# A test-time-training layer beside a mixture-of-experts gate on one core: expert slots spread over the scan, the first half's output norm moved into it, the ending's evacuations split

## What is computed

```
xn = layernorm(x)                                   # x: 4 x 256 tokens x 256 channels
XQ, XK, XV = xn @ q_w.T, xn @ k_w.T, xn @ v_w.T     # 32 heads of 8, minibatches of 16 tokens
# scan over 16 minibatches, carrying W1 (8x8) and b1 per batch and head
Z1 = xk @ W1 + b1
grad = ln_fused_l2_bwd(Z1, xv - xk, ln_w, ln_b)
Z1_bar = xq @ W1 - eta * tril(xq @ xk.T) @ grad + b1 - tril(eta) @ grad
W1, b1 = W1 - (last_eta * xk).T @ grad, b1 - sum(last_eta * grad)
out = xq + ln(Z1_bar)                               # per head
s = layernorm(out) * post_w + post_b, then @ o_w.T
g = silu(top-2 of 8 experts: down(up * silu(gate)))
x + s * g
```

## Time and profile before

| | us |
|---|---|
| runs, median of 3 | 278.29 (276.3 to 278.8) |
| the profiled execution, its own time | 279.46 |
| its span in the trace | 277.6 |
| VectorE busy | 211.3 (76%) |
| TensorE busy | 209.6 (75%), mean granted clock 0.865 |
| ScalarE, GpSimd busy | 138.2 (50%), 127.8 (46%) |

### The profile page before, as it was taken

One profiled execution on the slowest core, in us unless ns is written; L12 is line 12 of the kernel. 1 busy time (PEld: TensorE's weight loads), 2 busy tenths in 40 slices (PEclk: granted clock), 3 DMA queues, 4 the chain that ended last, 5 costly groups with the idle time before them and its releaser, 6 DMA issues.

```text
span 277.6 us, 5087 instructions
## 1 busy us (share of the span) xinstructions
PE 209.6 (75%) x1754; PEld 155.4 (56%) x1754; DVE 211.3 (76%) x546; ACT 138.2 (50%) x296; POOL 127.8 (46%) x173
## 2 busy tenths in 40 slices
PE   8318991069977995899299955995999799939663
PEld 6205561043656773778167643684777577828452
DVE  2999999996029499969948994959499998895312
ACT  2411663052492575187146707570567586873840
POOL 2356298066663294266226611663284373151034
PEclk9856998556999799799959997599699999986899
DMA  6992000300000300020030002000300160000011
GB/s 187 406 322 76 3 0 0 81 0 1 2 2 6 77 2 0 9 75 2 0 81 2 0 7 77 0 2 5 79 1 2 18 201 19 1 0 0 4 76 77
DMA packets 21706, 13.22 MB, mean 48 GB/s; under 512 B 10417, under 2 KB 20017, under 8 KB 21169
## 3 DMA queue, kind: packets, MB, share of 16 engines
q1 hardware_dynamic: 21168, 12.03, 14.3%
q10 hardware_dynamic: 512, 0.87, 1.0%
HBM read 11.02 MB, written 1.84 MB: 46 GB/s over the span
## 4 chain that ended last, share of the span: by engine, by line
DVE 39%; PE 34%; ACT 14%; issue 7%; POOL 2%; DMA 2%; DVEq 0%; POOLq 0%; SPq 0%; ACTq 0%
PE bank L1055 10%; DVE dW L815 5%; DVE pr L810 5%; PE bank L976 5%; PE bank L1023 4%; DVE pr L749 4%; DVE bank L760 3%; ACT L504 3%; PE bank L1129 3%; PE bank L1075 3%; ACT upw L491 2%; DVE mif L714 2%; DMA small<-in_small 2%; ACT xqm L535 2%; PE bank L1103 2%
## 5 line engine op out<-in xcount | busy, mean ns | idle before, releaser
L1023 PE MATMUL bank<-xqm,xkT 32*32 32x128 f32 x512 | 22.8, 298 | 35.5 <-ACT A L474 20.0
L320 POOL TENSOR_TENSOR hh<-gate,upw 128x256 f32<-128x256 f32 x32 | 24.2, 759 | 49.4 <-ACT upw L491 49.3
L265 POOL TENSOR_TENSOR A<-A,mask 128x256 f32<-128x256 f32 x32 | 23.4, 734 | 47.7 <-ACT A L474 47.5
L1023 PEld LDWEIGHTS bank<-xqm,xkT 32*32 32x32 f32 x512 | 13.1, 113 | 45.2 <-ACT A L474 21.6
L474 ACT ACTIVATE A<-bank,one 128x256 f32<-128x256 f32 x32 | 15.1, 473 | 46.1 <-PE bank L1023 46.0
L1075 PE MATMUL bank<-down,hT 128*128 128x256 f32 x128 | 36.6, 414 | 0.0
L784 DVE RECIPROCAL bank<-sv 128x32 f32<-128x32 f32 x16 | 5.7, 358 | 35.6 <-ACT sv L480 35.2
L1055 PE MATMUL bank<-gup_hi,xn_hi 128*128 128x512 f32 x64 | 32.5, 508 | 0.0
L1055 PE MATMUL bank<-gup_hi,xn_lo 128*128 128x512 f32 x64 | 28.1, 438 | 0.0
L1055 PE MATMUL bank<-gup_lo,xn_hi 128*128 128x512 f32 x64 | 27.9, 437 | 0.0
L1075 PEld LDWEIGHTS bank<-down,hT 128*128 128x128 f32 x128 | 24.6, 214 | 2.3
(11 more groups left out here) (149 smaller groups left out, 485.4 us busy)
## 6 DMA issues: line engine op xcount, KB each, us to landing
wblk<-w_blocks SPq DMA_DIRECT2D x8, 512.0 KB, 4.0
sgpad<-in_gup SPq DMA_DIRECT2D x1, 1024.0 KB, 9.7
G<-in_gup SPq DMA_DIRECT2D x1, 1024.0 KB, 11.7
down<-in_down SPq DMA_DIRECT2D x1, 1024.0 KB, 14.3
xkT<-in_x_bt SPq DMA_DIRECT2D x1, 1024.0 KB, 4.7
out<-G SPq DMA_DIRECT2D x4, 256.0 KB, 2.5
wkv<-in_wkv ACTq DMA_DIRECT2D x1, 512.0 KB, 4.1
x_bt<-in_x_bt SPq DMA_DIRECT2D x1, 512.0 KB, 7.6
```

Source lines behind the costliest of these rows:

```text
L320: pool.tensor_tensor(hh[:, i % 2, :, :], gate[:, i % 2, :, :], upw[:, i % 2, :, :], ALU.mult).then_inc(S_["h"], 1)
L1023: ins = pe.matmul(bk[32 * b:32 * b + 32, P * hf:P * hf + P], xkT[32 * q:32 * q + 32, hf, j, GT * b:GT * b + GT], xqm[32 * q:32 * q + 32, j ...
```

## The change

SLOTS becomes 3 slots in group 1, 5 in groups 2 to 6, 4 in group 7: all 32 stand in the scan. Every group j now begins with a slot; group_end(j-1) follows tile 1, and group_start(j) stands behind tile 4 of its own group instead of in the next. ScalarE loads the Sqrt table ahead of scores 1 and takes the first root right behind them. On GpSimd pad_grads(j-1) comes first. In the start, xn_hi is cast and the second half's queries are evacuated before any score of group 0; lower_half is one instruction of 2,048 columns instead of four of 512; mif lies in PSUM. The first half's output norm is done in fills of groups 6 and 7 on VectorE, with its row scaling on GpSimd (first_half_rows) and its roots inside ScalarE's groups 6 and 7. In the ending VectorE evacuates the first half's channels and tiles 6 and 7, ScalarE tiles 4 and 5; f_bank names banks 2, 6, 4, 5. The semaphore yT is split in yTa (ScalarE) and yTv (VectorE).

```diff
 NE, NI = 8, 128
 NF = 2 * B
 NS = NF * NE // 2
-FIRST_HALF = [0, 2, 2, 3, 3, 3, 3, 3]
...
-        mif = sb("mif", [P, NF, 2])
+        mif = bank[3][:, 488:488 + 2 * NF].rearrange("p (f k) -> p f k", k=2)
...
-            return 2 + f % 4
+            return (2, 6, 4, 5)[f % 4]
...
                 pool.wait_ge(S_["hi"], n + 1)
-                for c in range(0, 2048, 512):
-                    pool.tensor_tensor(lo[:, c:c + 512].bitcast(F32R), full[:, c:c + 512], hi[:, c:c + 512],
-                                       ALU.subtract).then_inc(S_["split"], 1)
...
             lower_half(1)
-            pool.wait_ge(S_["mask"], 1)
-            mask_scores(0, 1)
             lower_half(2)
             masked_queries(1)
-            for i in range(2, 5):
+            pool.wait_ge(S_["mask"], 1)
+            for i in range(1, 5):
                 mask_scores(0, i)
...
+            def first_half_rows():
+
+                for k in range(2):
+                    pool.wait_ge(S_["zr"], k + 1)
+                    pool.wait_ge(S_["zg"], k + 1)
+                    rows = o[:, k, :].rearrange("p (a d) -> p a d", d=HD)
+                    link(pool.tensor_tensor(rows, rows, zr[:, k, :].unsqueeze(2).broadcast_to([P, 64, HD]), ALU.mult))
+                    pool.wait_ge(S_["xqb"], 2 * B)
+                    pool.tensor_tensor(o[:, k, :], o[:, k, :],
+                                       xqb[:, 0, 2 * k:2 * k + 2, :].rearrange("p b c -> p (b c)"), ALU.add).then_inc(S_["orow"], 1)
+
...
-                    half_scale(0)
+                slots = list(range(slot, slot + SLOTS[j]))
+                slot += SLOTS[j]
+                if j == 1:
+                    hidden_product(slots.pop(0))
+                    pad_grads(0)
+                else:
+                    pad_grads(j - 1)
+                    hidden_product(slots.pop(0))
+                mask_scores(j, 1)
...
-                    mask_scores(j, 1)
-                    hidden_product(slot)
                     mask_scores(j, 2)
-                    pad_grads(j - 1)
-                    mask_scores(j, 3)
-                    hidden_product(slot + 1)
+                    hidden_product(slots.pop(0))
                 else:
...
+                    hidden_product(slots.pop(0))
+                    mask_scores(j, 2)
+                mask_scores(j, 3)
+                hidden_product(slots.pop(0))
                 mask_scores(j, 4)
...
+                if 1 < j < 6:
+                    query_bias(2 * (j - 2))
+                if j == 5:
+                    half_scale(0)
+                for i in slots:
                     hidden_product(i)
-                if j < 5:
-                    query_bias(2 * (j - 1))
-                slot += SLOTS[j]
+                if j == 6:
+                    first_half_rows()
             pad_grads(NG - 1)
-            for i in range(slot, NS):
-                hidden_product(i)
-                if i == slot:
-                    half_scale(1)
+            half_scale(1)
...
+            high_half(2)
+            queries_out(1)
+            step_std(2)
+            query_rows(0)
+            query_rows(1)
...
+            for i in range(1, 5):
+                scores_out(0, i)
+            act.wait_ge(S_["wx"], 1)
             slot = 0
             for j in range(1, NG):
+                slots = list(range(slot, slot + SLOTS[j]))
+                slot += SLOTS[j]
+                expert_slot(slots.pop(0))
+                if j == 1:
+                    preload_sqrt(3)
+                    scores_out(1, 1)
+                    step_std(3)
+                    expert_slot(slots.pop(0))
+                    scores_out(1, 2)
+                else:
+                    preload_sqrt(2 * j)
+                    scores_out(j, 1)
+                    step_std(2 * j)
+                    scores_out(j, 2)
+                    if j == 4:
+                        half_out(0)
+                    if j == 6:
+                        norm_z(0)
+                    if j == 7:
+                        norm_o(0)
+                    expert_slot(slots.pop(0))
+                scores_out(j, 3)
+                expert_slot(slots.pop(0))
+                scores_out(j, 4)
                 if j > 1:
...
+                    preload_sqrt(2 * j + 1)
+                    step_std(2 * j + 1)
+                for i in slots:
                     expert_slot(i)
-                preload_sqrt(2 * j)
...
             act.wait_ge(S_["small2"], 16)
-            norm_z(0)
-            expert_slot(slot)
+            expert_slot(NS)
+            expert_slot(NS + 1)
+            preload_sqrt(0)
             half_out(1)
-            norm_o(0)
             norm_z(1)
-            for i in range(slot + 1, NS):
-                expert_slot(i)
-            post_rows(0)
-            expert_slot(NS)
-            post_rows(1)
             norm_o(1)
-            post_rows(2)
-            post_rows(3)
-            expert_slot(NS + 1)
-            for f in range(4, NF):
-                post_rows(f)
+            post_rows(4)
+            post_rows(5)
...
 
-            def group(j, ring, late=None, last=False):
...
+            def second_half_rows(k):
 
                 p0 = post_count
...
+                v.wait_ge(S_["zs"], 3 + k)
+                link(v.reciprocal(zr[:, k, :], zs[:, k, :]), S_["post0"], p0)
+                v.wait_ge(S_["zg"], 3 + k)
+                link(v.tensor_tensor(o[:, k, :].rearrange("p (a d) -> p a d", d=HD),
+                                     zg[:, k, :].rearrange("p (a d) -> p a d", d=HD),
+                                     zr[:, k, :].unsqueeze(2).broadcast_to([P, 64, HD]), ALU.mult), S_["post0"], p0)
+                link(v.tensor_tensor(o[:, k, :], o[:, k, :],
+                                     xqb[:, 1, 2 * k:2 * k + 2, :].rearrange("p b c -> p (b c)"), ALU.add), S_["post0"], p0)
+                row_stats(k)
+
+            def post_rows(f):
+
+                v.wait_ge(S_["yTp"], f + 1)
+                for k in range(KC):
+                    v.tensor_scalar(yT[:, f // B, k, :, f % B, :],
+                                    bank[f_bank(f)][:, P * k:P * k + P].rearrange("p (j t) -> p j t", t=GT),
+                                    post_w[:, k:k + 1], post_b[:, k:k + 1], ALU.mult, ALU.add).then_inc(S_["yTv"], 1)
...
+            def gate_rows(first, end):
+
+                for f in range(first, end):
...
-            def routes_and_inputs():
-                route_weights()
-                upper_half(2)
+            def routes_and_inputs(m, i):
+                if (m, i) == (0, 0):
+                    upper_half(2)
+                if (m, i) == (0, 1):
+                    route_weights()
 
             group(1, 1, routes_and_inputs)
             with v.Fori(0, 4, 2) as i:
...
-            group(6, 0)
-            group(7, 1, last=True)
-            half_variance(0)
-            half_out_rows(0)
+            def first_half_a(m, i):
+                if (m, i) == (0, 1):
+                    half_variance(0)
+                if (m, i) == (1, 1):
+                    first_half_factors()
+
+            def first_half_b(m, i):
+                if (m, i) == (0, 1):
+                    first_half_stats()
+                if (m, i) == (1, 1):
+                    half_normalise(0, 0)
+                    half_normalise(0, 1)
+
+            group(6, 0, first_half_a)
+            group(7, 1, first_half_b, last=True)
+            v.wait_ge(S_["small2"], 16)
+            for f in range(4):
+                post_rows(f)
             half_variance(1)
-            half_normalise(0)
-            half_out_rows(1)
-            half_normalise(1)
-            gate_rows()
+            gate_rows(0, 2)
+            second_half_rows(0)
+            second_half_rows(1)
+            gate_rows(2, 4)
+            half_normalise(1, 0)
+            half_normalise(1, 1)
+            post_rows(6)
+            post_rows(7)
+            gate_rows(4, NF)
...
-                pe.wait_ge(S_["yT"], 8 * (f // B + 1))
+                if f < B:
+                    pe.wait_ge(S_["yTv"], 8)
+                else:
+                    pe.wait_ge(S_["yTa"], 4)
+                    pe.wait_ge(S_["yTv"], 12)
...
-            tile(0, 1)
-            tile(0, 2)
-            tile(0, 3)
-            query_rows(0)
-            tile(0, 4)
             pe.wait_ge(S_["kchc"], 4)
             channels(wq, (0, 1), 1, "qch")
+            query_rows(0)
             query_rows(1)
+            tile(0, 1)
+            group_start(0)
+            for i in range(2, 5):
+                tile(0, i)
...
-                last = slot + SLOTS[j]
+                slots = list(range(slot, slot + SLOTS[j]))
+                slot += SLOTS[j]
+                expert_slot(slots.pop(0))
                 tile(j, 1)
                 if j == 1:
-                    group_start(0)
-                    tile(j, 2)
-                    tile(j, 3)
-                    expert_slot(slot)
-                    tile(j, 4)
```

(38 more changed lines are left out.)

106 lines of the change are left out of this document (31 added, 75 removed).

## The result

The changed kernel took 249.68 us (median of 4 runs, 248.07 to 250.22), beside 278.55 for the kernel before on the same chip (4 runs, 276.3 to 281.39). The ratio is 0.898, with a 95% interval of 0.890 to 0.906. The forecast was 244 with a range of 235 to 257. The profiled execution took 250.22 us for a span of 248.4, against 279.46 and 277.6 before; VectorE is busy 215.8 us of it (87%), TensorE 203.5 (82%, granted clock 0.89).

The account below looks back on a forecast made before the run. The prediction took the scan's chain on VectorE as the bound, with 35.2 us of waits for ScalarE's roots. Start -13.1, groups 2 to 6 -10.6 and end -10.9 gave -34.6, a span of 243.0, 244 us; range 235 to 257.

Parts of the forecast that it names:

- If TensorE is at half clock there, slot 0 is 1.2 later and this gives back 1: Second minibatch of group 1: a caveat of 1 us on the forecast gain of 13.1 to the start of group 2.
- Group 1 then starts at 45.1: Start: cast of mif to PSUM saves 5.0 us, merged lower_half delays the copy by 2.4; 45.1 instead of 47.8.
- A<-G and sv of group 1: Start: merged subtractions of GpSimd hold up VectorE's copy of G by 2.4 us and sv by 3.9.
- The opening of a group: Groups 2 to 6: one slot ahead of tile 1 removes the first minibatch's root wait; 21.65 us per group without a wait.
- Group 4: Scan: half_bias and the four half_out copies stand ahead of slot work and delay the second root, +1.9 us.
- Group 6: Scan: half_variance and two reciprocals of the first half's norm now lie inside it, +2.3 us.
- Group 2: Scan: pair rows for group 3 come late, +2.0 us, and the root behind them +0.6.
- The port in the loop: Groups 2 to 6: sv held by GpSimd's runs on the shared port, between 0 and 9 us in all, taken as 3.5.
- The end: Group 7 and the ending take 50.2 us against 61.1, with group 7 at 21.6: a gain of 10.9.
- ports: Rival, 20%: sv waits for the end of GpSimd's run each time, the cast or route_weights too; 251.5 us.
- TensorE sets the group: Rival, 13%: slot round trips cost each of five groups 2.4 us beyond TensorE's spare 1.1; 256 us.
- slower: Rival, 2%: TensorE at half clock throughout, a group of five slots takes 35 us; 311 us.

Follow-up runs that it names:

- after: The profiled execution of the changed kernel itself: 250.22 us for a span of 248.4; the kernel's median is 249.68 us.
- a_changed: The changed kernel without any edit, measured again as reference for a later set: 248.98 us, ratio 0.913 to the kernel before, span 246.6.
- i_warm_18: Changed kernel plus 18 matmuls of zeros in TensorE's pause before the second half's query rows: 245.57 us, ratio 0.897 to the kernel before.
- c_gap_psum: Changed kernel with the second largest logit copied to PSUM first, so gap has one operand in SBUF: 245.80 us, ratio 0.901 to the kernel before.
- b_split: Changed kernel with lower_half as four instructions of 512 columns again: 246.23 us, ratio 0.904 to the kernel before.
- e_old_opening: Changed kernel with groups 2 to 7 opening as before: tile 1 before the slot; scores, slot, table, root on ScalarE: 268.95 us, ratio 0.978.
- h_bias_early: Changed kernel with half_bias(0) moved from TensorE's group 4 to the end of its group 3: 244.96 us, ratio 0.891 to the kernel before.
- f_norm_at_end: Changed kernel with the first half's output norm behind the scan again: 258.44 us, ratio 0.941 to the kernel before.
- g_evac_scalar: Changed kernel with ScalarE alone evacuating all eight channel tiles of the ending: 252.41 us, ratio 0.919 to the kernel before.
- l_all_four: Changed kernel with lower_half in four, gap with one operand in PSUM, half_bias(0) early and 12 zero matmuls in TensorE's pause: 239.86 us, ratio 0.861.
- k_split_bias_warm: Changed kernel with lower_half in four, half_bias(0) at the end of group 3 and 12 zero matmuls in TensorE's pause: 244.43 us, ratio 0.866.

## Why the prediction was right in direction and 5.7 us low

By its own steps, in us of span (forecast, then "after"):

| piece | forecast | measured |
|---|---|---|
| start, to group 2 | 74.2 | 80.75 |
| groups 2 to 6 | 118.6 | 117.6 |
| group 7 and the end | 50.2 | 50.0 |
| span | 243.0 | 248.4 |

The whole miss is the first piece. Two steps of it were mis-sized: "If TensorE is at half clock there, slot 0 is 1.2 later and this gives back 1", and "Group 1 then starts at 45.1". What the runs put in their place:

- **Half clock in group 1.** A pause was foreseen, since the forecast has TensorE wait for the query rows, and the earlier trace rows had shown what follows such a pause. I charged 1.2 us, for one slot. It holds for everything until about 75 us: query rows 1.94 for 1.04, four tiles of 1.08 for 0.64, group_start 3.62 for 1.9. The wait that the late root made is 4.3 us in "after" and 2.7 in a_changed, where the clock came back for a few microseconds; in i_warm_18 it is gone, and group 2 opens 4.1 and 2.3 us sooner than in these two. The pair rows of group 2 are late too (3.1 of idle time, forecast 2.0), but 2.4 of that is left in i_warm_18, so the clock at the return doesn't explain most of it.
- **The gap subtraction.** Not in the forecast: I moved the cast out of GpSimd's way and did not ask which instruction stands ahead of it with operands in SBUF. It took 4.31 instead of 0.17, and group 1 opened at 48.7 instead of 45.1. c_gap_psum, without this alone, opened at 45.28, and its query rows ended at 55.35 (forecast 56.0, "after" 58.78): the stall had also made TensorE's pause 3.9 us longer. The median of c_gap_psum is 3.2 us below a_changed's, that of i_warm_18 3.4 (from another set); how far the two overlap was not measured by a run with these two edits alone.

What held:

- **A<-G and sv of group 1** behind the merged subtraction: 4.12 us to 40.09 (forecast 40.3) and 3.61 (forecast 3.9). b_split shows 2.11 and 0.35 with quarters; merging costs 2.5 of span (2.8 in the medians). That the first copy gets in after one quarter and others wait for all four, as the cast of the earlier trace rows did, was known to go both ways.
- **The opening of a group.** Groups 3 and 5 are 21.8 (forecast 22 to 23, with 21.65 for a group without a wait). e_old_opening gives 20.5 us of span back with this order alone. That is the change's core.
- **Group 4.** Forecast 1.9 over a plain group, measured 3.4. That half_bias stands ahead of the second root was right (h_bias_early removes 3.0 us of the wait and 2.6 of the group). Missing was the fall of TensorE's clock behind it, 1.3 us in group_end.
- **Group 6.** Forecast 2.3, measured 1.9 (23.6 against 21.65).
- **Group 2.** Forecast 2.6, measured 3.7 (25.4).
- **The port in the loop.** I took 3.5 of a possible 9, which was too much; sv lost 0.7, and groups 3 and 5, which have no other term, are 0.25 over the plain 43.3. The sum for groups 2 to 6 came out only 1.0 high because errors cancel: groups 2 and 4 were 1.1 and 1.5 too low, group 6 and the port 0.4 and 3.3 too high.
- **The end.** 28.7 behind the transpose for a forecast of 28.6, group 7 21.3 for 21.6. The projection took 5.63 (taken: 5.8). By f_norm_at_end the first half's norm inside the scan is worth 9.1 us of span, by g_evac_scalar the shared evacuation 2.7.

Undoing one part at a time gives 20.5 + 9.1 + 2.7 - 2.5 (the merging, which harms) = 29.8 us, where the whole change gave 24 to 29 (medians: 273.2 against 248.98 in one set, 278.55 against 249.68 in another). The runs of the parts come from different sets, and single parts need not add; the order of their sizes is what they show.

Of the signs named in the forecast these came true: the cast under 0.4, a clock above 0.95 in groups 2 to 6, A<-G over 3 us, and all but exactly the wait before the reciprocals (8.0 for "under 8") and the length of groups 3 and 5 (21.8 for 22 to 23). The last sgT at 219.1 lies outside 212 to 216, which is the miss in the start.

Of the rivals, "ports" named the right cause in the wrong place: gap was held in the start, while sv was not held group after group. "TensorE sets the group" did not come true at 95% busy: groups 3 and 5 lose nothing. It is near, though: two microseconds of half_bias ahead of a root, with the clock that fell behind it, showed as 3.4. Against "slower" the forecast had said that each fall of the clock followed a pause of over 2.5 us. That was misread: already in the kernel before the clock was 0.50 from 91 to 94 us after an idle time of 1.45, and the fall in group 4 of the changed kernel followed one of 1.41.

## What to carry to other kernels

When a change parks an engine for several microseconds, price everything it does after the pause at the lower clock, not the next instruction alone, and ask who waits at the end of that stretch. When an operation is moved out of a shared port's way, list the neighbours that still read two operands from SBUF; the next one may be held instead. When one execution of a kernel differs from another, compare them stretch by stretch before pricing an edit by its span. A long wait for a cheap instruction (here a root of 0.29 us) is worth following to what stands ahead of it in its engine's list: that order was most of the gain.

## What was not expected of the hardware

- An operation of 128 x 8 elements with both operands in SBUF was held 4.31 us by one GpSimd instruction and 4.88 us by a run of four; with one operand in PSUM it took 0.17 while such an instruction ran (c_gap_psum), and 0.17 when issued 0.08 us behind the start of such a run (l_all_four).
- VectorE can't rely on getting in at a boundary between two of GpSimd's instructions. A copy of 2,048 columns got in at the first (2.11 us, b_split), the next copy in the same kernel (2.74) and gap in k_split_bias_warm (4.88) waited for the end of four. The Trainium skill, page "SBUF — State Buffer", section "Who interferes with whom", says that whoever issues first gets the shared pair of ports for the whole instruction. These runs show the loser kept out longer than that one instruction. What tells the two cases apart is open.
- A group_start, 16 matmuls with a weight load of 128 x 32 each, took 1.93 us at full clock (i_warm_18) and 3.62 at half ("after").
- A matmul of zeros with 256 columns of f32 appeared as two records and took 0.436 us at full clock; 18 of them in a pause of 8.5 us kept the granted clock at 1.00 from 45 to 64 us (0.76 from 45 to 57 and 0.50 from 57 to 64 without). It fell to 0.50 behind that, for some 7 us.
- TensorE's clock fell with little idle time ahead of it: to 0.56 at 133 us in "after", behind 1.41 us of idle time, a tile and half_bias. In h_bias_early, where group_end doesn't stand behind half_bias, it stayed at 1.00.
